# Attention cores: the first group's score maxima in two halves of queries, its first four steps between the units of the second half

## What is computed

```python
q, k, v = heads(x @ Wq), heads(x @ Wk), heads(x @ Wv)      # 4 batches, 16 heads of 8 (or 4) features
scores = jnp.einsum('bhqd,bhkd->bhqk', q, k)
scores = jnp.where(causal, -jnp.inf, scores * scale)
w = jax.nn.softmax(scores, axis=-1)                        # needs the maximum over k of every query
out = jnp.einsum('bhqk,bhkd->bqhd', w, v) @ Wo + b
```

## Time and profile before

| | |
|---|---|
| median of the timed runs | 5800.48 us |
| the profiled execution | 5776.4 us |
| its span, first to last instruction | 5774.7 us |
| mean granted clock of TensorE (1 is 2.4 GHz) | 0.919 |
| busy share of the span: PE, DVE, ACT, POOL | 82, 66, 55, 29 % |
| starts of the five attention cores in the span (L1004) | 893.2, 1670.35, 2383.9, 3086.4, 4993.5 us |

### The profile page before, as it was taken

How to read it: one execution, slowest core, us unless ns; L and a number is a source line. 1 busy time by engine, 2 the same in 40 slices (tenths; PEclk the granted TensorE clock), 3 DMA queues, 4 the chain that set the end, 5 groups by cost and what they waited for, 6 DMA issues and landing times. The chain is left out here.

```text
span 5774.7 us, 90836 instructions
## 1 busy us (share of the span) xinstructions
PE 4735.2 (82%) x33596; PEld 2081.6 (36%) x33596; DVE 3787.2 (66%) x4596; ACT 3161.8 (55%) x6002; POOL 1684.7 (29%) x1468
## 2 busy tenths in 40 slices
PE   5677667998569977699776998589867799699999
PEld 2233224443223336233352333256422344233344
DVE  6899658886579943799437992677539710699410
ACT  5655444766438853388534885444466421388621
POOL 0666315886032225323152220000006400222100
PEclk8899888999779989799897999789989999799999
DMA  0000012221032225322253220000000000211100
GB/s 27 0 1 1 4 49 76 44 44 29 10 112 42 55 65 177 115 51 51 74 154 120 50 46 20 6 10 2 5 10 0 20 0 0 60 31 45 42 0 15
DMA packets 146884, 239.83 MB, mean 42 GB/s; under 512 B 37382, under 2 KB 66930, under 8 KB 145076
## 3 DMA queue, kind: packets, MB, share of 16 engines
q1 hardware_dynamic: 125748, 197.74, 12.8%
q10 hardware_dynamic: 15744, 28.32, 1.5%
q0 software_dynamic: 4992, 8.41, 0.6%
HBM read 153.93 MB, written 80.31 MB: 41 GB/s over the span
## 5 line engine op out<-in xcount | busy, mean ns | idle before, releaser
L946 ACT ACTIVATE l_core_probs<-l_core_ps_scores_b 128x512 f32<-128x512 f32 (+3 forms) x3840 | 1611.3, 510 | 570.7 <-PE l_core_ps_scores_b L862 415.6
L1046 DVE TENSOR_REDUCE l_core_chunk_max<-l_core_ps_scores_a 128x2 f32<-128x1024 f32 (+3 forms) x1280 | 1253.3, 1020 | 83.9 <-PE l_core_ps_scores_a L847 48.6
L862 PE MATMUL l_core_ps_scores_b<-l_q_rows_sb,l_k_rows_sb 64*128 64x512 bf16 (+3 forms) x3840 | 944.5, 333 | 32.2 <-ACT l_core_probs L946 9.7
L847 PE MATMUL l_core_ps_scores_a<-l_k_rows_sb,l_q_rows_sb 64*128 64x512 bf16 (+3 forms) x3840 | 740.2, 346 | 121.1 <-DVE l_core_chunk_max L1046 44.7
L995 POOL TENSOR_SCALAR_AFFINE_SELECT l_core_probs<-l_core_probs 128x512 f32<-128x512 f32 x512 | 325.4, 636 | 1161.4 <-ACT l_core_probs L946 1156.4
L877 PE MATMUL l_core_ps_acc<-l_core_probs,l_v 128*9 128x512 f32 (+3 forms) x6144 | 647.7, 494 | 16.0 <-ACT l_core_out_sums L928 9.0
L862 PEld LDWEIGHTS l_core_ps_scores_b<-l_q_rows_sb,l_k_rows_sb 64*128 64x128 bf16 x3840 | 304.0, 94 | 690.0 <-ACT l_core_probs L946 607.9
L1046 DVE TENSOR_REDUCE l_core_neg_max<-l_core_ps_scores_a 128x2 f32<-128x256 f32 (+3 forms) x640 | 493.4, 819 | 84.8 <-PE l_core_ps_scores_a L807 83.0
L1917 POOL TENSOR_TENSOR l_scan_bx<-l_xs,l_scan_b_rows 128x1024 f32<-128x1024 f32 x192 | 452.3, 2356 | 224.2 <-DVE l_scan_states L1927 217.8
L1927 DVE TENSOR_TENSOR_SCAN l_scan_states<-l_scan_ps_decay,l_scan_bx 128x1024 f32<-128x1024 f32 x192 | 439.7, 2290 | 40.8 <-POOL l_scan_bx L1917 15.3
L965 POOL TENSOR_TENSOR l_core_probs_decayed<-l_core_probs,l_decay 128x1536 f32<-128x1536 f32 (+2 forms) x160 | 394.0, 2487 | 142.9 <-ACT l_core_probs L946 142.9
(11 more groups left out here) (323 smaller groups left out, 7711.9 us busy)
## 6 DMA issues: line engine op xcount, KB each, us to landing
l_slots_weights<-m_both_dram SPq DMA_DIRECT2D x78, 512.0 KB, 4.7
l_k_rows<-l_proj_parts ACTq DMA_DIRECT2D x96, 256.0 KB, 5.3
l_q_rows<-l_proj_parts SPq DMA_DIRECT2D x96, 256.0 KB, 5.1
l_q_rows_sb<-l_q_rows SPq DMA_DIRECT2D x128, 192.0 KB
l_k_rows_sb<-l_k_rows SPq DMA_DIRECT2D x128, 192.0 KB
l_heads_out<-l_core_out_sums SPq DMA_DIRECT2D x300, 32.0 KB
l_core_heads<-l_heads_out SPq DMA_DIRECT2D x15, 512.0 KB, 5.6
l_core_inverse_rows<-l_rsums SPq DMA_DIRECT2D x15, 512.0 KB, 7.0
```

Of the source, the lines that this page charges most:

```text
L847: mm = nc.tensor.matmul(slot[:, i, 0:w], qs[n % 3][rows, p, qt * P:(qt + 1) * P], ks[n % 3][rows, p, c * NT:c * NT + w], start=True, stop= ...
L862: mm = nc.tensor.matmul(pb[m % 3][:, 0:w], ks[n % 3][rows, p, kt * P:(kt + 1) * P], qs[n % 3][rows, p, q0:q0 + w], start=True, stop=not diag)
L946: nc.scalar.activation(pt[:, ts % RP, j, 0:w], pb[m % 3][:, 0:w], ACT.Exp, scale=scale).then_inc(b_free, 1)
L1046: nc.vector.tensor_reduce(to, pa[e % 2][:, :, 0:width_a(qt, c)], AX.X, ALU.max, negate=True).then_inc(a_free, 1)
```

## The change

For group 0 alone, the eight units of query tiles 0 to 3 (`HALF_A`) get a transpose entry of their own, (0, NA + 1), two units later, of 16 rows, from a new tile `neg_max_first`. The second half's entry stays where the group's entry stood, also of 16 rows. Each entry has its own round of copy, split and DMAs, six small DMAs instead of three. PE starts the steps after 18 entries (`START_A`) rather than after 35 (33). Steps 0 to 3 follow the plan with the units a that come next; before step 4, PE runs all entries up to `DONE_A[0] + a`, and waits for the rows of the second half. POOL splits the second half's maxima after it has cut the diagonal of step 3. From step 4 on the order is the old one. The diff, cut to its core:

```diff
+    HALF_A = sum(1 for qt, p, c in UNITS_A if qt < 4)
...
+            if (n, k) == (0, HALF_A + TURN_AT):
+                ORDER_A.append((0, NA + 1))
             ORDER_A.append((n, k))
...
+    START_A = ORDER_A.index((0, 2 * HALF_A + 1))
...
+                def first_rows(half):
+                    sp.wait_ge(mp_ready, half + 1)
+                    for e in range(3):
+                        for p in range(2):
+                            sp.dma_start(qs[0][r0 + e:r0 + e + 65:64, p, half * NT:(half + 1) * NT],
+                                         mpart[8 * p:8 * p + 8, e, :]).then_inc(m_in, 16)
...
-                max_rows(0)
+                first_rows(0)
+                first_rows(1)
...
-                for e in range(DONE_A[0]):
+                for e in range(START_A):
                     unit_a(e)
-                e = DONE_A[0]
+                e = START_A
...
-                    pe.wait_ge(m_in, MIN * (n + 1))
+                    pe.wait_ge(m_in, rows_in(n + 2 if n else 1))
...
                         elif kind == "b":
+                            if n == 0 and b == 16:
+                                while e < DONE_A[0] + a:
+                                    unit_a(e)
+                                    e += 1
+                                pe.wait_ge(m_in, rows_in(2))
                             unit_b(n, b // 4, b % 4)
...
                         if t == 8 and n + 1 < GROUPS:
-                            max_parts(n + 1)
+                            max_parts(n + 2)
+                        if ts == 3:
+                            max_parts(1)
...
                     if k == NA - 1:
                         dve.wait_ge(a_free, e + 1)
-                        nc.vector.tensor_tensor(nm[:, n % 2, :, :, 4:8], mc[:, n % 2, 0, :, :, :], mc[:, n % 2, 1, :, :, :],
-                                                ALU.min).then_inc(nm_ready, 1)
+                        for p in range(1 if n else 2):
+                            to = nm[:, n % 2, :, :, 4:8] if n else nm0[:, 1, p, :, :]
+                            by = slice(None) if n else p
+                            both = nc.vector.tensor_tensor(to, mc[:, n % 2, 0, :, by, :], mc[:, n % 2, 1, :, by, :], ALU.min)
+                        both.then_inc(nm_ready, 1)
```

More of the change, by code:

```diff
@@ L706, in attn_core @@
         nm = sb("neg_max", [P, 2, 2, 2, 8])
+        nm0 = sb("neg_max_first", [P, 2, 2, 2, 4])
         mc = sb("chunk_max", [P, 2, 2, 2, 2, 4])
@@ L736, in attn_core @@
         CIN = 16 * (6 + 6 + (6 if alibi else 0) + (2 if decay else 0))
-        MIN = 16 * 3
+        rows_in = lambda s: 16 * (6 * min(s, 2) + 3 * max(0, s - 2))
+        m_rows = lambda s: 16 if s < 2 else 32
         with nc.Block() as block:
@@ L834, in unit_a @@
                         return
+                    if n == 0 and k >= NA:
+                        if k == NA + 1:
+                            pe.wait_ge(a_free, HALF_A)
+                        else:
+                            pe.wait_ge(nm_ready, 1)
+                        nc.tensor.transpose(slot[0:16, 0, 0:P], nm0[:, NA + 1 - k, :, :, :].rearrange("p i h k -> p (i h k)"),
+                                            net.ident[:, :]).then_inc(a_ready, 1)
+                        return
                     if k == NA:
@@ L1041, in chunk_max @@
                     qt, p, c = UNITS_A[k]
-                    to = nm[:, n % 2, :, p, qt] if qt < 4 else mc[:, n % 2, c, :, p, qt - 4]
+                    if qt >= 4:
+                        to = mc[:, n % 2, c, :, p, qt - 4]
+                    else:
+                        to = nm[:, n % 2, :, p, qt] if n else nm0[:, 0, p, :, qt]
                     dve.wait_ge(a_ready, e + 1)
-                    if k == 0 and n >= 2:
+                    if k == 0 and n >= 3:
                         dve.wait_ge(a_ready, ORDER_A.index((n - 2, NA)) + 1)
@@ L1053, in max_parts @@
+                        both.then_inc(nm_ready, 1)
                 def max_parts(e):
-                    n = ORDER_A[e][0]
-                    t = pa[e % 2][0:32, 0, 0:P]
+                    n, k = ORDER_A[e]
+                    s = n + 1 if k == NA else 0
+                    rows = slice(0, m_rows(s))
+                    t = pa[e % 2][rows, 0, 0:P]
                     dve.wait_ge(a_ready, e + 1)
                     if not decay:
-                        if n:
-                            dve.wait_ge(mp_ready, n)
-                        nc.vector.tensor_copy(mcopy[:, :], t).then_inc(mc_ready, 1)
-                        dve.wait_ge(mc_ready, n + 1)
+                        if s:
+                            dve.wait_ge(mp_ready, s)
+                        nc.vector.tensor_copy(mcopy[rows, :], t).then_inc(mc_ready, 1)
+                        dve.wait_ge(mc_ready, s + 1)
@@ L1062, in max_parts @@
                         dve.sem_inc(a_free, 1)
                         return
-                    if n:
-                        dve.wait_ge(m_in, MIN * n)
-                    nc.vector.tensor_copy(mpart[:, 0, :], t).then_inc(m_chain, 1)
-                    dve.wait_ge(m_chain, 2 * n + 1)
-                    nc.vector.tensor_tensor(mrest[:, :], t, mpart[:, 0, :], ALU.subtract).then_inc(a_free, 1)
+                    if s:
+                        dve.wait_ge(m_in, rows_in(s))
+                    nc.vector.tensor_copy(mpart[rows, 0, :], t).then_inc(m_chain, 1)
@@ L1069, in max_parts @@
+                    dve.wait_ge(m_chain, 2 * s + 1)
+                    nc.vector.tensor_tensor(mrest[rows, :], t, mpart[rows, 0, :], ALU.subtract).then_inc(a_free, 1)
                     dve.wait_ge(a_free, e + 1)
-                    nc.vector.tensor_copy(mpart[:, 1, :], mrest[:, :]).then_inc(m_chain, 1)
-                    dve.wait_ge(m_chain, 2 * n + 2)
-                    nc.vector.tensor_tensor(mpart[:, 2, :], mrest[:, :], mpart[:, 1, :], ALU.subtract).then_inc(mp_ready, 1)
+                    nc.vector.tensor_copy(mpart[rows, 1, :], mrest[rows, :]).then_inc(m_chain, 1)
@@ L1074, in _ @@
+                    dve.wait_ge(m_chain, 2 * s + 2)
+                    nc.vector.tensor_tensor(mpart[rows, 2, :], mrest[rows, :], mpart[rows, 1, :],
+                                            ALU.subtract).then_inc(mp_ready, 1)
                 for e in range(len(ORDER_A)):
@@ L1084, in _ @@
                         late(e, *LATE[k])
-                    elif k == NA:
+                    elif k >= NA:
                         max_parts(e)
```

27 lines of the change are left out of this document (15 added, 12 removed).

## The result

The changed kernel took 5815.52 us (median of 22 runs, 5806.6 to 5821.67), the kernel before 5803.85 us (22 runs on the same chip). The ratio is 1.0018, 95% interval 1.0012 to 1.0024: slower by 10.4 us, 7 to 14. The slowdown is clear of noise and lies just inside the 0.2% bound that the prediction set.

A forecast was written before the change was run, and what follows sets the result against it. The prediction took DVE's reductions to bound each core's opening. Four cores without decay at +3.0 us (+12.0) and +4.7 with decay gave +16.7 us, put on the median of 5800.48: 5817 us, range 5799 to 5830.

The forecast's parts named there:

- case A: The forecast itself: the clock falls in the block of units before step 4; 5817 us (5808 to 5830), chance 0.83.
- DVE's terms: Per core without decay, up to step 4: idle time -0.7 us (0 to -1.35), second copy +0.6, second joining operation +0.2.
- the first wait: PE's wait for the first half's rows before step 0: +0.4 us (0 to +1.5) per core without decay, +0.2 with decay.
- What bounds the opening: Each core's opening is bound by DVE's reductions, busy 29.15 of 31.69 us; they set step 4's start in both kernels.
- DVE's idle time in steps 0 to 3: In steps 0 to 3, DVE's 1.35 us of idle time would halve: -0.7 us a core (0 to -1.35).
- the added copy: Second copy on DVE in a core without decay: 0.28 us plus 0.33 us waiting for the next unit, +0.6.
- the joins: Second joining operation on DVE: +0.2 us without decay; with decay, slowed beside POOL's multiplying, +2.6 us (0.2 to 3.8).
- The first rows: The first half's rows land about 1687.3; unit 17 comes 0.4 us late, first exponential 17 to 18 us after core start.
- The clock: Falls to 0.50 in the block; slow steps from step 4 cost 0.46 x 5.5 = +2.5 us a core (+1.6 to +3.8).
- Rival B: The clock holds through the block, as PE never stands still longer than about 1 us; 5805 us, chance 0.12.
- The core with decay: Its opening: extra round +1.1, idle -1.0 and -0.7, first rows +0.2, clock +2.5, joining beside POOL +2.6; sum +4.7 us.

The follow-up runs named there:

- spread_block: The changed kernel with six of the block's units moved from before step 4 to behind the second half's units of steps 4 to 11; ratio 1.0024 to the kernel before.
- two_queues: The changed kernel with three of the first half's six small DMAs issued by ACT's queue instead of all by SP; ratio 1.0018 to the kernel before.
- block_twice: The changed kernel with the two main matmuls of each unit in the block before step 4 made twice; ratio 1.0023 to the kernel before.
- block_fill: The changed kernel with an extra full-array fp32 matmul ahead of each longer unit in the block before step 4; ratio 1.0047 to the kernel before.
- one_join: The changed kernel with group 0's two joining operations made one; ratio 1.0025 to the kernel before.
- before_fill: The kernel before with extra full-array fp32 matmuls in the opening's units of 512 columns, from the seventh unit; ratio 1.0076 to the kernel before.
- before_warm: The kernel before with the main matmuls of the last ten units ahead of the steps (eight with decay) made twice; ratio 1.0000 to the kernel before.

## Why the prediction was right or wrong

The cause and the sign were right (case A). The size was 16.7 us against 10.4 measured. The likeliest class, slower by over 0.2%, was just missed, and the range, 5799 to 5830, holds both the 5815.5 us measured and 5800.48 x 1.0018 = 5810.9.

One sum is off: the upper ends of DVE's terms and of the first wait add up to +2.3 a core (0 + 0.6 + 0.2 + 1.5), not +1.5, and the range would then end at about 5834. The measured time is far from it.

**What bounds the opening**: right. DVE's reductions set when step 4 starts, with the steps early or late: 40.41 and 40.72 us in the second core, and six units fewer before step 4 (spread_block) only move time from one side of it to the other.

**DVE's idle time in steps 0 to 3**: wrong where the steps ran at half clock. I counted on -0.7 us. Steps 0 to 3 in cores 2 and 5, from their first matmul to the start of their last, and the block of core 2 (columns as above):

```profile
1690.73:1700.31 9.58, 9.13 (x60) 2.95 (x61) 8.30 (x8) 5.62 (x14) 1.91 (x3) 0.55 0.00 0
5051.07:5059.34 8.27, 7.06 (x61) 2.59 (x62) 7.97 (x8) 5.57 (x14) 1.84 (x3) 0.79 0.00 0
1700.31:1715.61 15.30, 8.62 (x95) 3.79 (x92) 14.10 (x21) 0.45 (x2) 2.03 (x5) 0.69 0.01 2
```

In core 2 DVE is idle for 1.28 us, where I had 1.35 before; in core 5, where the clock rose during the steps, only for 0.30, and for 0.16 in cores 2 to 5 of two_queues. So the gain came only where the clock was up. In the stretches of units alone DVE's idle time grew: 2.54 us before (31.69 - 29.15), 1.96 and 1.20 now. Of these 0.6 us more, 0.3 is the wait at the added copy, which I had counted; the rest I had put at nothing. Idle time up to step 4 rose from 3.89 to 4.44 us. The copy cost 0.57 (taken as 0.6), and the joins 0.24 together in the core without decay (0.34 predicted, 0.17 each). In all, DVE's terms and the first wait came to +0.3 us a core up to step 4 in the mean of the profiles, +0.5 predicted.

**The first rows**: right in kind and nearly in size. The first exponential came 16.48 us after the start, half a microsecond ahead of the 17 to 18 predicted, and two_queues shows the rows late for PE by 0.3 us, where I had 0.4. Step 4's first exponential was to come 0.5 us later than before: +0.6, +0.3 and +0.3 in cores 2 to 4, against the first profile of before. In core 5 it came 0.9 us sooner than in the first profile of before and 0.4 later than in the second; there the clock had risen 19.1 us after the core's start, 2.9 us into the steps, and the rest of steps 0 to 3 ran at 1.00.

**The clock**: the mechanism was right, and this is the term that was mis-sized. It fell in the block in every core of every run that has one. The two factors were 0.46 of each microsecond and 5.5 us. The first held: 1 - 1.93 / 3.30 = 0.42 over step 4. The second did not: the clock stayed low for 2.5 to 4.3 us behind step 4's first exponential (3.41 in the second core), and beyond step 4 it cost nearly nothing. The cores lost 1.34, 1.32, 1.34 and 1.21 us over 3.41, 2.98, 4.32 and 2.46 us at 0.50. In block_twice 1.28 us cost 0.60 and 1.70 us 0.81; in core 5 of block_fill, where it was at 1.00 but for the first 0.1 us, nothing was lost. So the loss grows by 0.42 to 0.49 us for each microsecond, up to some 3 us, and then stays at 1.2 to 1.5. The longest case is the second core of two_queues, with 5.27 us at 0.50 behind step 4's first exponential: it lost 1.53, and its step 5, at a mean clock of 0.62, took 2.62 us where a later group takes 2.39. My working let the loss grow to 2.5, because I priced all the time at half clock by a step that PE bounds (step 2), and step 5 has room. Four cores at 1.3 instead of 2.5 are 4.8 us less. That is most of the error in the cores without decay: 12.0 us predicted, 6.4 measured (the mean of the two profiles of after less that of before: 1.8, 2.1, 1.5 and 0.9 us in cores 2 to 5).

Rival B's premise, that a clock is kept where PE never stands still for long, is refuted: in the second core PE's longest wait from the first step to step 4 was 1.1 us, and the clock fell. PE's waits in that stretch of the second core (us in total, times, longest):

```profile
PE l_core_ps_scores_a L869 <- DVE l_core_chunk_max L1081: 4.8, 7, 1.1
```

By the rule of the Trainium skill's page "TensorE: Matmul & The Clock Gate", section "HAM oscillation — how this bites in real kernels", the clock is lost in long stretches without matmuls; this trace disagrees with that as the only way to lose it.

**The core with decay**: +4.7 predicted, and 65.3 - 60.6 = +4.7 measured in the mean of the profiles, but that is luck, since it comes from other parts. The joins of group 0 took 1.77 us where the one join took 0.17 before: +1.6, predicted +2.6. The 0.96 us of DVE idle that was to vanish came back as 1.29, since the plan now has matmuls of a step and their masks, at half clock, ahead of the unit that DVE wants next. And step 4 lost 2.0 us: half of it the clock's (1.0 instead of the 2.5 predicted), half a wait of PE for DVE's reduction, which my sum put at nothing. Here the total was right by parts that cancelled. That the joins are slow only beside POOL is in line with the Trainium skill's page "SBUF — State Buffer", section "Who interferes with whom", by which an operation of VectorE with both inputs in SBUF contends with one of GpSimd that reads SBUF, for a port that one of them holds exclusively; one_join's 1.71 us for one operation, which ends 0.03 us after POOL's product, agrees with it.

## What to carry to other kernels

Work that is moved to an earlier time wins nothing if the engine that bounds the stretch does the same work by the stretch's end; add up that engine's busy and idle time to the point where the two orders meet before counting a gain. In this kernel a block that left PE waiting for DVE handed the next stage a half clock and no unit in hand. The price of the clock is to be taken from the steps that PE itself bounds, step by step, since those with room absorb it. Matmuls added to keep the clock up cost far more than it gave back in block_fill and before_fill, where they met the low clock themselves; in block_twice and before_warm they won nothing.

## What was unexpected of the hardware

- The clock fell with PE busy 67% of 10.25 us, of doubled matmuls on 64 rows (block_twice), and rose in the second core of before_fill only after 30.6 us at 76%. In one core of block_twice it held for 20 us, in the others for 7 to 10, over the same units. In the changed kernel the first rise came 18.4 to 24.4 us after the core's start, and in the kernel before core 5's opening differed by 1.3 us between two profiles with a rise that came 3.6 us sooner.
- A join beside POOL's product lasted until that product ended: 1.71 us for one, 1.77 for two in a row. In the later round of the same core, when POOL was multiplying again, a cast of 32x128 in SBUF took 2.12 us and ended 0.1 us after a product (in the kernel before it took 2.12 too), where the first half's of 16x128 took 0.22 with POOL at rest. The cast that reads PSUM, 0.6 us ahead of it and beside the same product, took 0.28.

```profile
920.19 0.22 DVE L1110 CAST l_core_max_parts<-l_core_max_rest 16x128 bf16<-16x128 f32 x1
...
948.39 2.12 DVE L1110 CAST l_core_max_parts<-l_core_max_rest 32x128 bf16<-32x128 f32 x1
```
